# Cross-attention stage: where the sums over the exponentials are made, and in which order GpSimd makes the next norms

## What is computed

```
x = x + self_attn(layernorm(x))          # 16 heads; each row is attended over the 4 batch entries
x = x + cross_attn(layernorm(x), ctx)    # 16 heads of 32, 128 context tokens per batch entry
x = x + ffn(layernorm(x))                # 512 -> 64, relu over 16 inner units each, -> 512

cross_attn: scores = q k^T / sqrt(32), masked; attn = softmax(scores, axis=-1); out = attn v, then Wo
```

## Time and profile before

| | |
|---|---|
| median of 3 runs | 1825.08 us (1824.74 to 1825.36) |
| the profiled execution's own time | 1824.81 us |
| its span in the trace | 1823.0 us, mean granted TensorE clock 0.972 |
| `cross_block` in the trace | 858 us to the end; 16 steps, 56.9 us each in the steady part |
| busy share over the whole span | PE 92%, DVE 84%, ACT 59%, POOL 56% |
| instructions of the exponentials (L1493) | 1024 ACTIVATE, 1024 ACTIVATION_READ_ACCUMULATOR |

### The profile page before, as it was taken

One profiled execution on the slowest core, in us unless ns is written; L12 is line 12 of the kernel. 1 busy time (PEld: TensorE's weight loads), 2 busy tenths in 40 slices (PEclk: granted clock), 3 DMA queues, 4 the chain that ended last, 5 costly groups with the idle time before them and its releaser, 6 DMA issues.

```text
span 1823.0 us, 37774 instructions
## 1 busy us (share of the span) xinstructions
PE 1686.1 (92%) x13848; PEld 1392.5 (76%) x13848; DVE 1523.1 (84%) x2097; ACT 1083.7 (59%) x3456; POOL 1018.6 (56%) x721
## 2 busy tenths in 40 slices
PE   6899999999999999963799999999999999999996
PEld 5778888888888888842577777778777787777874
DVE  6798888888888888773478998889988899888887
ACT  4434444444444444322567887778877788777884
POOL 3167777766666777673344645546455464544521
PEclk9999999999999999986799999999999999999997
DMA  5401111111111111042011110111101112011101
GB/s 212 136 24 47 41 34 43 46 46 46 46 46 46 46 46 47 24 81 77 24 44 50 61 60 26 60 61 61 64 23 61 61 61 64 21 61 61 38 25 47
DMA packets 72794, 98.76 MB, mean 54 GB/s; under 512 B 22208, under 2 KB 30528, under 8 KB 72640
## 3 DMA queue, kind: packets, MB, share of 16 engines
q1 hardware_dynamic: 71056, 96.09, 16.2%
q10 hardware_dynamic: 1584, 0.61, 0.2%
HBM read 59.66 MB, written 37.03 MB: 53 GB/s over the span
## 4 chain that ended last, share of the span: by engine, by line
PE 27%; ACT 12%; DVE 9%; issue 5%; ACTq 0%; DVEq 0%
PE ring L1269 12%; ACT prob_c L1493 10%; DVE g_sb L1617 5%; PE sc L1297 5%; PE ring L1274 3%; PE ring L1309 3%; PE ring L1356 2%; PE sc L1289 2%; PE sc L1269 1%; DVE q L1804 1%; ACT relu L1473 1%; DVE g_sb L1614 1%; DVE gT L1627 1%; ACT gT L1483 1%; ACT pT L1461 1%
## 5 line engine op out<-in xcount | busy, mean ns | idle before, releaser
L412 PE MATMUL qb<-wqkv,xT 128*128 128x512 f32 x2304 | 551.3, 393 | 6.1 <-DVE wqkv L869 6.1
L412 PEld LDWEIGHTS qb<-wqkv,xT 128*128 128x128 f32 x2304 | 429.5, 189 | 93.5 <-DVE wqkv L869 6.3
L1493 ACT ACTIVATE prob_c<-sc,ntop 128x128 f32<-128x128 f32 x1024 | 363.4, 391 | 8.2 <-DVE ntop L1645 6.5
L1221 POOL TENSOR_TENSOR rstd<-vare,half_c 128x1 f32<-128x1 f32 x64 | 35.1, 549 | 456.6 <-DVE vare L1699 456.6
L1493 ACT ACTIVATION_READ_ACCUMULATOR prob_c<-sc,ntop 128x1 f32 x1024 | 235.7, 230 | 0.0
L330 POOL TENSOR_TENSOR prod_pool<-v,prob 128x1024 f32<-128x1024 f32 x64 | 180.6, 2822 | 74.7 <-DVE prob L795 69.5
L1269 PE MATMUL ring<-wqkv,aT_c 128*128 128x512 f32 x768 | 193.5, 401 | 10.5 <-DVE aT_c L1600 9.6
L501 PE MATMUL ob<-wout,aT 128*128 128x512 f32 x768 | 192.0, 399 | 11.2 <-DVE aT L825 11.2
L581 ACT ACTIVATE v<-qb 128x512 f32<-128x512 f32 x64 | 38.4, 599 | 260.3 <-PE qb L412 251.8
L1269 PE MATMUL ring<-xT_c,wqkv 128*128 128x512 f32 x768 | 185.4, 401 | 1.5 <-DVE xT_c L1600 1.5
L581 ACT ACTIVATE qk<-qb 128x512 f32<-128x512 f32 x128 | 76.1, 596 | 177.1 <-PE qb L412 177.1
(11 more groups left out here) (137 smaller groups left out, 3349.8 us busy)
## 6 DMA issues: line engine op xcount, KB each, us to landing
x_tile<-in_x SPq DMA_DIRECT2D x16, 1024.0 KB, 5.3
x_scratch<-xres SPq DMA_DIRECT2D x16, 1024.0 KB, 4.5
x_tile<-x_scratch SPq DMA_DIRECT2D x16, 1024.0 KB, 5.2
out<-x SPq DMA_DIRECT2D x64, 256.0 KB, 2.0
kt<-k_scratch SPq DMA_DIRECT2D x16, 512.0 KB, 3.2
v_c<-v_scratch SPq DMA_DIRECT2D x16, 256.0 KB, 3.6
raw<-in_wqkv SPq DMA_DIRECT2D x3, 1024.0 KB, 8.8
ctx<-in_ctx SPq DMA_DIRECT2D x1, 1024.0 KB, 8.4
```

Source lines behind the costliest of these rows:

```text
L412: last = nc.tensor.matmul(qb[g % 4][:, :], xT[p][a][:, k, t * P:(t + 1) * P], wqkv[b][:, k, c * D:(c + 1) * D], start=(n == 0), stop=(n == ...
L1493: last = nc.scalar.activation(prob[:, h, :], sc[g][:, (h % 4) * C:(h % 4 + 1) * C], ACT.Exp, bias=ntop[:, h:h + 1], accum_out=total[:, t % ...
```

## The change

Four things. ScalarE's exponentials no longer have the accumulator output. GpSimd makes the sums instead, by a tree: per tile two additions that fold the two halves of `prob_c` (8 heads each, 64 columns) into a new buffer `part`, five additions in place over all 16 heads of 32, 16, 8, 4 and 2 columns, and one of the last two columns into `total_c`. GpSimd's stream is put in a new order: for each tile t the sums `totals(t)`, then `norm(t)`, then `norm2(j, t + 1)`; the four residuals follow behind tile 3. Two waits are new outside GpSimd: `exps(t, g)` waits until the halves of `prob_c` that it overwrites have been folded, and `normalise(t)` waits for the sums of tile t-1 from GpSimd rather than for ScalarE. The sums are now in the order of the slots of `prob_c`, so the reciprocal reads and writes through a rearranged view.

```diff
--- before.py
+++ after.py
@@ -1104,6 +1104,7 @@
         x2T = [sb(f"x2T{h}", [P, DK, 4 * P], F32R) for h in range(2)]
         relu = sb("relu", [P, 4, 4 * P])
         g_sb = sb("g_sb", [P, 4 * P])
+        part = sb("part", [P, H, C // 2])
         gT = [sb(f"gT{h}", [P, 4 * P], F32R) for h in range(2)]
         ntop = sb("ntop", [P, H])
         total = sb("total_c", [P, 2, H])
@@ -1125,6 +1126,7 @@
         xm_done, xn_done, res_done = (sem(f"c_{n}") for n in ("xm", "xn", "res"))
         bn2_done, mv2_done, var2_done, rstd2_done, x2m_done, xn2_done, bf_added = (
             sem(f"c_{n}") for n in ("bn2", "mv2", "var2", "rstd2", "x2m", "xn2", "bf_added"))
+        added, halved, tree = sem("added"), sem("halved"), sem("tree")
         scored, topped, exped, summed = sem("scored"), sem("topped"), sem("exped"), sem("summed")
         relu_done, hinged, g_hi, g_lo = sem("relu_done"), sem("hinged"), sem("g_hi"), sem("g_lo")
         hinge_ready = sem("hinge_ready")
@@ -1230,22 +1232,36 @@
                         nc.gpsimd.tensor_tensor(at, at, rstd2[:, 0:1].to_broadcast([P, D]), ALU.mult).then_inc(xn2_done, 1)
                     nc.gpsimd.tensor_tensor(x2[pp][:, tt, :], x2[pp][:, tt, :], bf[:, :], ALU.add).then_inc(bf_added, 1)
 
+                def totals(t):
+                    if not has(j):
+                        return
+                    over = 4 * j + t
+                    wait(pool, added, over)
+                    for half_ in range(2):
+                        heads = slice(8 * half_, 8 * half_ + 8)
+                        wait(pool, exped, 16 * j + 4 * t + 2 * half_ + 2)
+                        nc.gpsimd.tensor_tensor(part[:, heads, :], prob[:, heads, 0:C // 2], prob[:, heads, C // 2:C],
+                                                ALU.add).then_inc(halved, 1)
+                    wait(pool, halved, 2 * over + 2)
+                    for n, width in enumerate((32, 16, 8, 4, 2)):
+                        wait(pool, tree, 5 * over + n)
+                        nc.gpsimd.tensor_tensor(part[:, :, 0:width], part[:, :, 0:width], part[:, :, width:2 * width],
+                                                ALU.add).then_inc(tree, 1)
+                    wait(pool, tree, 5 * over + 5)
+                    wait(pool, summed, over - 1)
+                    nc.gpsimd.tensor_tensor(total[:, t % 2, :], part[:, :, 0], part[:, :, 1], ALU.add).then_inc(added, 1)
+
+                for t in range(R):
+                    totals(t)
+                    if has(j, 1):
+                        if t == 0:
+                            wait(pool, x1_in, 32 * (j + 2))
+                        norm(t)
+                    if t < 3:
+                        norm2(j, t + 1)
                 if has(j, 1):
-                    wait(pool, x1_in, 32 * (j + 2))
-                    norm(0)
-                    norm(1)
-                norm2(j, 1)
-                if has(j, 1):
-                    norm(2)
-                    norm(3)
-                norm2(j, 2)
-                if has(j, 1):
-                    residual(0)
-                    residual(1)
-                norm2(j, 3)
-                if has(j, 1):
-                    residual(2)
-                    residual(3)
+                    for t in range(R):
+                        residual(t)
                 norm2(j + 1, 0)
 
             nc.gpsimd.memset(half[:, :], -0.5)
@@ -1489,10 +1505,10 @@
                     wait(act, psum["pT"], 16 * j + 4 * t - 3 + g)
                     if g == 0:
                         wait(act, taken["pv"], 4 * j + t - 1)
+                    wait(act, halved, 2 * (4 * j + t - 1) + (2 if g > 1 else 1))
                     for h in range(4 * g, 4 * g + 4):
                         last = nc.scalar.activation(prob[:, h, :], sc[g][:, (h % 4) * C:(h % 4 + 1) * C],
-                                                    ACT.Exp, bias=ntop[:, h:h + 1],
-                                                    accum_out=total[:, t % 2, head_of(h):head_of(h) + 1])
+                                                    ACT.Exp, bias=ntop[:, h:h + 1])
                     last.then_inc(exped, 1)
 
                 def prob_hi(j, i):
@@ -1702,9 +1718,10 @@
                     if not active(j, "pv", t):
                         return
                     over = TURNS_OVER["pv"](j, t)
-                    wait(dve, exped, 4 * over)
+                    wait(dve, added, over)
                     wait(dve, taken["pv"], over - 1)
-                    nc.vector.reciprocal(rtotal[:, :], total[:, (t - 1) % 2, :]).then_inc(summed, 1)
+                    nc.vector.reciprocal(rtotal[:, :].rearrange("p (m g) -> p g m", g=4),
+                                         total[:, (t - 1) % 2, :].rearrange("p (g m) -> p g m", g=4)).then_inc(summed, 1)
                     wait(dve, summed, over)
                     wait(dve, psum["pv"], over)
                     wait(dve, psum["aT"], over - 1)
```

## The result

The changed kernel takes 2042.8 us (median of 4 runs, 2042.2 to 2044.6), the kernel before 1825.2: the ratio is 1.119, with a 95% interval of 1.1175 to 1.1202. The prediction was 2050, its range 1970 to 2145.

What follows compares the result with a forecast made beforehand. PE was taken to bound the step. 13.3 + 2.7 - 0.7 = 15.3 us a step, 214 for fourteen steps, about 11 for the first and 1 for the last: 1824.8 + 226 = 2051, stated as 2050 us, range 1970 to 2145.

Steps and rivals of the forecast that it cites:

- GpSimd's price: GpSimd's additions for one tile's sums: 2.5 us for both halves and 3.7 for the tree, 6.2 us in all.
- The rival in which each run of an operand costs by itself: GpSimd's eight additions take some 17 us more a tile, 70 us a step, about 2900 in all; chance 0.04.
- The chain: GpSimd's sums, norms and norm2 in order end norm(3) at 51.5 instead of 38.2: PE loses 13.3 us a step.
- The round: One tile's work on GpSimd: sums 6.2, norm 2.1 and norm2 3.9, 12.2 us, where a tile took PE 9.9.
- The waits ahead of it: PE waits for the second norm's xn2 before norm_T(3): 1 us in tile 1 and near 3 in tile 2.
- The clock: PE runs at the lower clock after ten idle microseconds: 2.7 us a step, with ends 0 and 5.3.
- 18.7 + 2.7 - 0.7: PE from norm_T(3) to the next step: 18.7 us, plus 2.7 for lower clock, less 0.7 for vanished gT and prob_T waits.
- ScalarE: Without accumulator reads a head costs 0.25 us instead of 0.34, 1.4 a tile; tile 0's exponentials end at 7.5, not 8.8.
- Rival 5: ScalarE keeps 0.34 us a head, delaying GpSimd's start by 1.3 us a step: 2070 us in all; chance 0.03.
- First and last steps: The first step with a next block pays about 11 us, the last step, which has no norms, about 1.
- GpSimd's residuals and norm2 beside the hinges: Near VectorE's hinges the norms move away but these come near; PE's queries are then the longer chain: nothing.

Runs made afterwards that it cites:

- two reorderings: The changed kernel with all four norms ahead of tile 0's sums, 1880.1 us; and with norm(t) ahead of its own tile's sums, 1958.6 us.
- the run without a tree: The changed kernel without the five additions of 32 to 2 columns: 1888.7 us, ratio 1.035.
- the filled step: A step of the changed kernel with 36 constant-weight matmuls ahead of TensorE's wait for norm 3: 2029.0 us, ratio 1.112.
- the sum-free kernel: The kernel before with ScalarE's accumulator output left out and nothing in its place: 1800.7 us, ratio 0.987.
- the run with both sums: The changed kernel with ScalarE's accumulator output kept as well, into a tile that nobody reads: 2054.9 us, ratio 1.127.
- the first experiment: The changed kernel with all four norms of the next block made ahead of tile 0's sums: 1880.1 us, ratio 1.031.

## Why the prediction was right

By its own steps:

- **GpSimd's price.** A tile's sums were put at 6.2 us and are 6.1 (fold at 1256.04, norm at 1262.18). The line through two rows held down to 16 columns: 0.73, 0.46, 0.32, 0.24, 0.22 us against 0.73, 0.45, 0.31, 0.24, 0.21 by 0.17 + 2.19 ns a column. The rival in which each run of an operand costs by itself is gone: 16 runs of 1 to 32 columns cost what their columns cost. The Trainium skill's "GPSIMD Engine Reference", section on performance pitfalls, has about 102 cycles for each small read command. As a price for each run of an operand this trace doesn't bear it out: an addition with 16 runs of one column in each operand took 0.22 us.
- **The chain.** The round was put at 12.2 and is 12.1; norm 3 was to be out at 51.5 and TensorE starts on it at 51.8. Two small errors offset each other here: the chain starts 0.6 us late (see ScalarE below), and three rounds are 0.1 shorter each. The two reorderings and the run without a tree show that this is the cause and not only where the time appears.
- **The waits ahead of it.** Here a detail was wrong: I gave TensorE 1 us of waiting in tile 1 and near 3 in tile 2; it waits 1.64 and then, in the step shown, not at all. The 0.64 more in tile 1 are the late start of the chain. The clock was down behind the 1.64, and TensorE spent in slow matmuls what it would have waited; in the step from 951.53, where the clock stayed up behind 1.76, it then waited 2.63 in tile 2, as forecast. That made no difference to the sum, since GpSimd sets the end.
- **The clock.** 2.7 us a step were expected for the stretch behind norm_T(3). That stretch was put at 18.7 + 2.7 - 0.7 = 20.7 and is 19.8; the clock's part, by the filled step, is 2.1. This is the term that was mis-sized, by 0.6 us. The other 0.3 of the stretch's 0.9 stays open. With norm 3 some 0.3 us later than worked out, a step came out 0.6 us below the forecast, 8 us in the fourteen full steps, which is more than the 7 us by which the total was too high. I had taken the clock's price from 48 query matmuls, which began cold; here transpositions and ffn_in are the cold ones.
- **ScalarE.** The saving per head was right: an ACTIVATE follows its predecessor every 0.25 to 0.26 us (four end 1.14 us after the first starts), and the sum-free kernel gains 1.5 us a step, just above the 1.1 to 1.4 stated. What it does for the chain was overrated. Tile 0's exponentials were to end at 7.5, four heads behind the last maxima; the maxima are there at 6.5 as worked out, but ScalarE is then still at the third group of four, and the exponentials end at 8.1. Rival 5 prices the same term at 1.3 us a step; the run with both sums shows 0.9.
- **First and last steps.** Put at 11 and 1, measured from scores(0) to scores(0) 64.5 against 55.5 for the first, 9 more; from the last scores(0) to the end 86.8 against 86.9, nothing. Against these 3 us too many stand 2.1 that were in no term: the stage's first scores(0) starts at 886.99 instead of 884.85, as its first transposition already does (862.72 instead of 860.70), before any of the sums. In the runs that share the changed kernel's sums it starts at 884.1 to 885.5, so this is nothing that the change does in every execution.

So the chain and its prices were right. That the total came as near as it did (226 us more were forecast, 217 measured) is partly luck: 8 and 3 us too many, 2.1 too few.

One sentence of the sum was right without having been priced: that GpSimd's residuals and norm2 beside the hinges come to "nothing". Rows of GpSimd and VectorE in the step shown above:

```profile
1296.12 1.60 POOL L1233 TENSOR_TENSOR x<-x,bf 128x512 f32<-128x512 f32 x1
```

```profile
1296.01 0.55 DVE L1630 TENSOR_SCALAR g_sb<-relu,hinge,b 128x512 f32<-128x512 f32 x1 [3.17 <-ACT relu L1489]
```

The hinges hang on TensorE's ffn_in and so shift with it: the first stands 0.7 us behind the start of the queries here and in the kernel before. GpSimd begins its residuals at 1288.56, when norm 3 is out and TensorE goes on, and is done with norm2 1.7 us after the first hinge starts; before, it is busy for 5.7 us beside them, to 1217.11. So the queries are indeed the longer chain. In the two kernels that only move the norms forward GpSimd's tail lies deeper in the hinges, and this term comes up: with all norms first it runs to 55.0 of the step, the hinges begin at 43.0. I had read the row that shows it without pricing it.

## What to carry to other kernels

When a step is put into an in-order stream, look for the last instruction behind it that another engine takes in order, and compare the two times: here norm 3 was wanted at 38.2 and came at 51.8. With cheaper sums it still came at 41.5, too late, while the full sums behind the norms cost 56 us instead of 217. Before work is moved to an engine that is half idle, see where in the step its idle time is, and what its neighbour runs there: 3.8 us of additions cost nothing in one gap of GpSimd and 43 us in all in another. And price what the move can save by the waits of the bounding engine (1.5 us a step), not by the instructions removed (5.9).

## What the runs showed of the hardware that I had not expected

- How much GpSimd and VectorE slow each other: a hinge, two operands in SBUF, takes 0.75 us alone and 1.29 to 1.31 on average with GpSimd's two-operand additions beside it; those went from 1.24 to 1.66 each (three in 4.97 us). VectorE's operation on q, which reads one operand from PSUM, stays at 0.73 to 0.75 in the same stretch. The first hinge, which reads one tensor from SBUF, isn't always spared: in the changed kernel it takes 0.55 us in the step shown and 1.60 to 1.64 in seven others, each time beside the same two operations of GpSimd's norm2. Why these differ stays open.
- How short a gap can be followed by the lower clock. It fell behind 1.64 us of idle time in tile 2 of the changed kernel, and behind 2.11 in the filled one. But not each time: the gap of 2.98 in the first experiment's step was followed by mask rows of 0.51 us, at the usual length, and in another step of the filled kernel the same 1.64 us wait (for the transposition at 1250.23) by the same.
